# Sums of squares of the queries in the second cross attention: from VectorE's reductions to ScalarE's accumulator

## The reference

```python
def _ln(x, w, b):
    mu = jnp.mean(x, axis=-1, keepdims=True)
    var = jnp.mean(jnp.square(x - mu), axis=-1, keepdims=True)
    return (x - mu) * jax.lax.rsqrt(var + EPS) * w + b          # EPS = 1e-05

qx = _fp8_linear_pertensor(ln_out, wqx, wqx_scale, qx_in_scale).reshape(b, s, g, hpg, d)
qx = _ln(qx, qxln_w, qxln_b)            # 16 heads of d = 128, normed head by head
kx, vx = jnp.split(jnp.einsum('bsi,oi->bso', cond, w_kv_x), 2, axis=-1)
kx = _ln(kx.reshape(b, sc, g, d), kxln_w, kxln_b)               # 8 key heads
xout = _gqa(qx, kx, vx.reshape(b, sc, g, d)).reshape(b, s, nh * d)
```

## Time and profile before

| | |
|---|---|
| median of 3 runs | 3761.35 us (3760.2 to 3762.09) |
| profiled execution, its own time | 3757.82 us |
| profiled execution, span | 3756.0 us |
| PE busy over the span | 3468.4 us, 92% |
| VectorE (DVE) busy | 2306.6 us, 61% |
| ScalarE (ACT) busy | 1871.6 us, 50% |
| GpSimd (POOL) busy | 81.3 us, 2% |
| mean granted clock of PE | 0.974 of full speed |

### The profile page before, as it was taken

How to read it: one execution, slowest core, us unless ns; L and a number is a source line. 1 busy time by engine, 2 the same in 40 slices (tenths; PEclk the granted TensorE clock), 3 DMA queues, 4 the chain that set the end, 5 groups by cost and what they waited for, 6 DMA issues and landing times. The chain is left out here.

```text
span 3756.0 us, 75463 instructions
## 1 busy us (share of the span) xinstructions
PE 3468.4 (92%) x25760; PEld 2295.1 (61%) x25760; DVE 2306.6 (61%) x5644; ACT 1871.6 (50%) x5135; POOL 81.3 (2%) x133
## 2 busy tenths in 40 slices
PE   7999999999979989888886999999999999987799
PEld 4666666666653345566763666666666666665555
DVE  4555555555541146588876777777777777766832
ACT  4656566565636642266653544545444444534421
POOL 0000000000000000000000000000000000000000
PEclk9999999999999999999997999999999999998899
DMA  4111111111110010000002111111111111101000
GB/s 134 51 42 50 42 50 50 42 50 42 51 59 7 1 67 28 11 1 0 0 1 93 43 34 42 34 42 34 42 34 34 42 34 42 35 26 48 1 9 14
DMA packets 111935, 137.48 MB, mean 37 GB/s; under 512 B 11216, under 2 KB 90704, under 8 KB 110672
## 3 DMA queue, kind: packets, MB, share of 16 engines
q1 hardware_dynamic: 111824, 136.04, 11.3%
HBM read 133.65 MB, written 2.36 MB: 36 GB/s over the span
## 5 line engine op out<-in xcount | busy, mean ns | idle before, releaser
L393 PE MATMUL x_Kb<-x_cT,x_wk 128*128 128x257 f32 x3072 | 769.3, 385 | 12.1 <-ACT x_sq L646 8.8
L393 PEld LDWEIGHTS x_Kb<-x_cT,x_wk 128*128 128x128 f32 x3072 | 556.0, 191 | 183.5 <-issue 93.6
L430 PE MATMUL x_PC<-x_pT,x_cn 128*128 128x512 f32 x1024 | 473.7, 605 | 4.0 <-DVE x_pT L931 0.8
L666 ACT ACTIVATE x_pr<-x_pr,x_ntop 128x257 f32<-128x257 f32 x512 | 261.1, 510 | 303.5 <-DVE x_ntop L911 162.9
L646 ACT ACTIVATE x_sq<-x_Kb 128x257 f32<-128x257 f32 x512 | 195.7, 382 | 305.2 <-DVE x_kT L894 300.3
L430 PEld LDWEIGHTS x_PC<-x_pT,x_cn 128*128 128x128 f32 x1024 | 184.5, 190 | 243.0 <-issue 241.0
L894 DVE TENSOR_SCALAR x_kT<-x_Kb,x_vecs 128x257 f32<-128x257 f32 x512 | 244.2, 482 | 96.5 <-PE x_Kb L393 90.9
L412 PE MATMUL x_Sb<-x_kT,x_qT 128*32 128x257 f32 (+1 forms) x4096 | 275.6, 383 | 4.9 <-DVE x_pr L914 3.3
L672 ACT ACTIVATE x_pr<-x_pr,x_rps 128x257 f32<-128x257 f32 x512 | 241.3, 500 | 47.4 <-DVE x_rps L924 47.1
L377 PE MATMUL x_PC<-x_wq,x_xnT 128*128 128x512 f32 x512 | 242.7, 608 | 11.8 <-DVE x_wq L819 8.9
L931 DVE COPY x_pT<-x_PTb 128x512 f32<-128x512 f32 x256 | 176.6, 690 | 118.7 <-PE x_PTb L422 116.7
(11 more groups left out here) (299 smaller groups left out, 5645.0 us busy)
## 6 DMA issues: line engine op xcount, KB each, us to landing
x_cT<-in_ctxT SPq DMA_DIRECT2D x128, 257.0 KB, 2.8
x_cn<-in_ctx SPq DMA_DIRECT2D x128, 256.0 KB, 3.0
x_last<-x_last_row SPq DMA_DIRECT2D x128, 256.0 KB, 3.8
x_wq<-in_x_wq SPq DMA_DIRECT2D x2, 2048.0 KB, 7.8
x_wo<-in_x_wo SPq DMA_DIRECT2D x2, 2048.0 KB, 15.6
e_w<-in_e_w SPq DMA_DIRECT2D x3, 1152.0 KB, 7.7
c_staged_heads<-in_c_wqk SPq DMA_DIRECT2D x2, 1536.0 KB, 9.6
x_last_row<-x_last_rows SPq DMA_DIRECT2D x128, 2.0 KB
```

The lines of the kernel that those rows point to most:

```text
L393: m = pe.matmul(Kb[j % 2][:, 0:SE], wk[:, c, g * HD:(g + 1) * HD], cT[:, b, c, :], start=c == 0, stop=c == HC - 1)
L430: m = pe.matmul(PC[h][:, :], cn[:, b, c, h * P:(h + 1) * P], pT[:, c, :], start=c == 0, stop=c == KC - 1)
L666: act.activation(pr[:, v, :], pr[:, v, :], ACT.Exp, bias=ntop[:, u:u + 1], scale=1.0 if L1 else -1.0, accum_out=ps[:, u:u + 1]).then_inc(e ...
```

## The change

For layer 1 only, ScalarE no longer squares a group of four heads in one instruction of 512 columns. It squares each head in an instruction of 128 columns with `accum_out`, which leaves the sum of the squares in `qss`. VectorE's four reductions a tile (L882) are left out. `q_sq` has no use in layer 1, and `q_sum` is primed and incremented by ScalarE instead of VectorE.

```diff
         @block.scalar
         def _(act):
-            for s in (xt_copied, q_sq, q_log, q_rs, qt_copied, k_sq, k_log, k_rs, e_done, pn_done, ln_log, ln_rs):
+            (q_sum if L1 else q_sq).prime(act)
+            for s in (xt_copied, q_log, q_rs, qt_copied, k_sq, k_log, k_rs, e_done, pn_done, ln_log, ln_rs):
                 s.prime(act)
...
             def square_query(t, k):
                 act.wait_ge(q_in.sem, q_in.now(t, k + 1))
+                if L1:
+                    act.wait_ge(q_sum.sem, q_sum.after(t, k - 1))
+                    for h in range(4 * k, 4 * k + 4):
+                        a = act.activation(qsq[:, k % 2, h % 4, :], qn[:, h, :], ACT.Square,
+                                           accum_out=qss[:, h:h + 1])
+                    a.then_inc(q_sum.sem, 1)
+                    return
                 act.wait_ge(q_sum.sem, q_sum.after(t, k - 1))
                 act.activation(qsq[:, k % 2, :, :], qn[:, 4 * k:4 * k + 4, :], ACT.Square).then_inc(q_sq.sem, 1)
...
-            for s in (xn_done, xq_done, q_in, q_sum, qn_done, s_read, top_done, r_done, pt_copied, pc_copied,
+            if not L1:
+                q_sum.prime(dve)
+            for s in (xn_done, xq_done, q_in, qn_done, s_read, top_done, r_done, pt_copied, pc_copied,
                       oq_steps, o_copied, y_read, ln_sum, ln_agg, xq_steps, last_turned):
                 s.prime(dve)
...
             def sum_queries(t, k):
+                if L1:
+                    return
                 dve.wait_ge(q_sq.sem, q_sq.now(t, k + 1))
                 dve.tensor_reduce(qss[:, 4 * k:4 * k + 4], qsq[:, k % 2, :, :], AX.X, ALU.add).then_inc(q_sum.sem, 1)
```

## The result

| | before | after |
|---|---|---|
| median, us | 3761.23 (3760.2 to 3762.09) | 3851.27 (3849.11 to 3855.91) |
| profiled execution, its own time | 3757.82 | 3850.01 |
| span | 3756.0 | 3848.2 |
| VectorE busy | 2306.6 | 2274.0 |
| ScalarE busy | 1871.6 | 1911.1 |

A fourth run of before puts its median at 3761.23 instead of 3761.35. After takes 1.0241 times as long, with a 95% interval of 1.0228 to 1.0254: 90 us more. The direction was forecast, the size was not; 18.6 us were forecast, and the range ended at +25.

The account below looks back on a forecast made before the run. PE was taken to bound the kernel, busy 82.00 of 84.77 us a tile. ScalarE's 1.28 us in each of 15 tiles (19.2), less 0.6 ahead of the loop, gave 18.6 on 3761.35: 3780.0 us, range 3768 to 3786.

Parts of the forecast that it names:

- Price of a group on ScalarE: Four squares and accumulator reads on ScalarE's list take 1.16 us instead of 0.52, so 0.64 us more a group.
- What reaches PE: Slots 0 and 1 each pass 0.64 us to PE: 1.28 us a tile, 19.2 us in 15 tiles.
- one slot only: Rival: cover in slot 0 or a gap in slot 1's chain takes one delay; 3770 us, chance 0.12.
- hidden in both: Rival: ScalarE's extra time reaches PE in neither slot, only the head of the stage moves; 3761 us, chance 0.08.
- no overlap: Rival: accumulator reads on ScalarE don't overlap the next square; four heads cost 2.0 us, 3806 us, chance 0.05.
- What goes: VectorE's four reductions, 2.7 us a tile in slots 1 and 2, save nothing, since VectorE then waits for PE.
- faster: Rival: the reductions were the late link, so leaving them out saves 38 us in 15 tiles; 3742 us, chance 0.05.
- Ahead of the loop: Norms begin earlier, at about 2017.1 instead of 2017.77, and PE's transposes follow: -0.6 us, bounds 0 and -1.0.
- Sum of these: 19.2 - 0.6 = 18.6 us more, set on the median of 3761.35: 3780.0 us.
- The gain is nothing: Leaving out VectorE's reductions gains nothing in slots 1 and 2; if the cover failed, up to 1.27 us a pair.
- shift as a whole: Slots 2 and 3 hold no query squares, so their lists only move later, with no cost of their own.
- 86.05 us instead of 84.77: Test for the next profile: the time of a tile; the forecast is wrong if it stays under 85.3.

Follow-up runs that it names:

- e1: The changed kernel with six extra semaphore increments in VectorE's list just ahead of the loop; 3781.23 us, 1.0054.
- e4: The kernel before with ScalarE's accumulating squares alone, sums to a spare tile, VectorE's reductions kept; 3780.27 us, 1.0051.
- e8: The changed kernel with five extra semaphore increments in VectorE's list ahead of the loop; 3782.69 us, 1.0053.
- e6: The kernel before with VectorE's reductions left out, a constant for the sums, old squares, and six increments ahead of the loop; 3763.11 us, 1.0003.
- e11: The changed kernel with 192 extra semaphore increments in VectorE's list ahead of the loop; 3852.90 us, 1.0246.
- e2: The changed kernel with three extra semaphore increments in VectorE's list ahead of the loop; 3853.01 us, 1.0243.
- e3: The kernel before with eight key-column copies ahead of the loop made one, seven VectorE instructions fewer; 3838.45 us, 1.0201.
- e9: The changed kernel with four extra semaphore increments in VectorE's list ahead of the loop; 3855.30 us, 1.0251.

## Why the prediction was right and wrong

- **Price of a group on ScalarE**: 1.16 forecast, 1.17 measured. **What reaches PE**: 1.28 us a tile forecast; 1.28 in e1, e4 and e8, and in e1 at the places that were forecast. Tiles 1 and 14 got less, 0.95 and 1.02 (e1 against before). The rivals "one slot only", "hidden in both" and "no overlap" fall with it.
- **What goes**: right as to the work done (e6, 1.0003). The rival "faster" is refuted. The Trainium skill (Perfetto Trace Analysis, Identifying the Most-Contended Engine) ranks by occupancy, and the prediction had set that rule beside this rival; it did not hold here.
- **Ahead of the loop**: -0.6 forecast. From the start of the last query copy to the norms there were 3.30 us; after has 2.53 (2017.24 to 2019.77), so -0.77. But nothing of it is left at the end of tile 0. From VectorE's first mean of the query weights to the copy of `qT` in tile 0 there are 100.73 us before, 102.07 in e6 and 102.99 in e1. In e6, where ScalarE's squares are the old ones, the lower clock in slot 1 goes with it (windows under e6). So tile 0 cost 2.26 us in e1, where the forecast had 1.28 - 0.6.
- **Sum of these**: 3780.0 forecast, 3780.3 to 3782.7 measured in e1, e4 and e8. That it is so near is in part luck: tile 0 cost 1.6 us more than its share of the sum, and tiles 1 and 14 together 0.6 less.
- **What failed**: the step "The gain is nothing" took an instruction that is left out to cost nothing at worst, and slots 2 and 3 to "shift as a whole". Both looked at time only. Leaving instructions out also shifts the loop in VectorE's list, and none of the rivals had that: 70.0 us (after against e1), or 78% of the loss. The range could not hold it. Neither the rows of before nor its 46 packets on the instruction queue gave the price, and the packets say something only beside the 107 of after.
- Of the tests named for the next profile, that of the tile ("86.05 us instead of 84.77") did its work: first 85.91 and last 85.62 are near it, the 12 others are not. That pattern, tiles of the loop against tiles written out, is what pointed to the jump.

What stays open: the wait of e6 at place 1850, why the wait behind the jump is 2.8 to 3.0 us in e11 and 2.2 to 2.5 in the others, and whether anything but the granted clock adds to the 1.81 us behind PE's wait.

## What to carry to other kernels

An edit that changes how many instructions an engine runs ahead of a loop, or in it, can move the loop across an edge of the blocks in which instructions are fetched. To see it, compare tiles inside the loop with tiles written out, look for waits by "issue" behind the jump, and compare the packets of the instruction queue. If they differ, pad ahead of the loop with instructions that do nothing before judging the edit itself: here the edit itself cost 19 us and the loop's place 70 us. Less work on VectorE helped nothing here, since it idled next, but the place of the work on ScalarE's list did: the same squares, moved behind another key, turned +19 into -7 us, each against its own runs of before.

## What the runs showed that I had not expected

- One instruction that does nothing, ahead of a loop of 329, changes the time by 73 us (3782.69 against 3855.30).
- A jump back into a block that isn't held costs VectorE 2.2 to 2.5 us, the next block 1.5 to 2.4 us more, together 3.7 to 4.9 (after, e2, e3, e9). Where only the loop's end crosses an edge (e11) it is 2.8 to 3.0 us behind the jump and 0.4 at the end.
- PE, after 4.66 us of idle time, was granted 0.50 of its clock for about 5 us, which added 1.8 us to the 4.0 that it had waited.
